# A graph network's edge phase on one core: first layer formed transposed in PSUM, the loop written out, one fp32 matmul for the segment sum

## What is computed

```python
edge_feat = jnp.concatenate([x[src], x[dst], edge_attr], axis=-1)   # 512 + 512 + 64
h = mish(edge_feat @ W1 + b1)                                       # x * tanh(softplus(x))
messages = mish(h @ W2 + b2)
agg = jax.ops.segment_sum(messages, dst, num_segments=x.shape[0])
```

## Time and profile before

| | |
|---|---|
| median of 3 runs | 1525.7 us (1524.73 to 1533.9) |
| the profiled execution's span | 1537.4 us, mean granted TensorE clock 0.889 |
| edge phase in it | from 116.4 us (L758, the table load) to 1176.9 us (first instruction of the node phase) |
| busy, whole span | PE 1222.1 us (79%), DVE 1091.5 (71%), ACT 895.1 (58%), POOL 923.7 (60%) |

### The profile page before, as it was taken

How to read it: one execution, slowest core, us unless ns; L and a number is a source line. 1 busy time by engine, 2 the same in 40 slices (tenths; PEclk the granted TensorE clock), 3 DMA queues, 4 the chain that set the end, 5 groups by cost and what they waited for, 6 DMA issues and landing times. The chain is left out here.

```text
span 1537.4 us, 21831 instructions
## 1 busy us (share of the span) xinstructions
PE 1222.1 (79%) x5491; PEld 929.1 (60%) x5492; DVE 1091.5 (71%) x1793; ACT 895.1 (58%) x1061; POOL 923.7 (60%) x1006
## 2 busy tenths in 40 slices
PE   0981788898888888888888888888894999559972
PEld 0751566666666666666666666666663777448861
DVE  3631587887988887888779777877887587663364
ACT  2211677777767776777677767767774454143341
POOL 1325687778778777887777878777743111064420
PEclk9995899989999999999899999989996999579975
DMA  4524444444444544544444444444431011363443
GB/s 135 198 103 89 103 95 94 95 83 101 87 88 91 96 89 84 100 95 87 96 88 92 98 87 87 91 91 93 90 82 55 8 40 43 103 162 114 130 150 119
DMA packets 113342, 147.33 MB, mean 96 GB/s; under 512 B 55389, under 2 KB 63980, under 8 KB 113225
## 3 DMA queue, kind: packets, MB, share of 16 engines
q0 software_dynamic: 40912, 101.69, 31.3%
q1 hardware_dynamic: 72377, 45.20, 10.7%
q10 hardware_dynamic: 16, 0.02, 0.0%
HBM read 136.29 MB, written 15.66 MB: 99 GB/s over the span
## 5 line engine op out<-in xcount | busy, mean ns | idle before, releaser
L896 PE MATMUL ps<-W2h,hTh 128*128 128x512 f32 x664 | 294.6, 444 | 74.5 <-ACT hTh L775 68.7
L730 POOL DMA_INDIRECT gath<-dst_table,idx_sl x166 | 285.1, 1718 | 41.7 <-issue 41.5
L896 PE MATMUL ps<-W2l,hTh 128*128 128x512 f32 x664 | 285.8, 430 | 0.0
L896 PEld LDWEIGHTS ps<-W2h,hTh 128*128 128x128 f32 x664 | 137.7, 207 | 138.8 <-ACT hTh L775 82.9
L718 POOL DMA_INDIRECT gath<-src_table,idx_sl x166 | 184.3, 1110 | 58.3 <-issue 55.2
L748 POOL TENSOR_TENSOR msg_lo<-act,msg_hi 128x1024 fp32r<-128x1024 f32 x83 | 199.6, 2404 | 31.3 <-DVE msg_hi L842 30.0
L769 ACT ACTIVATE act<-ps 128x1024 f32<-128x1024 f32 x83 | 85.0, 1024 | 206.8 <-POOL msg_lo L748 145.2
L866 DVE TENSOR_TENSOR agg<-agg,ps 125x512 f32 x166 | 113.7, 685 | 96.6 <-PE ps L940 85.6
L896 PE MATMUL ps<-W2h,hTl 128*128 128x512 f32 x664 | 168.3, 395 | 0.0
L706 POOL TENSOR_TENSOR e_carrier<-e_carrier 1x1 f32<-1x1 f32 x249 | 90.5, 363 | 119.6 <-DMA idx_sl<-idx_scr 88.9
L896 PEld LDWEIGHTS ps<-W2l,hTh 128*128 128x128 f32 x664 | 138.9, 209 | 30.5
(11 more groups left out here) (319 smaller groups left out, 2853.6 us busy)
## 6 DMA issues: line engine op xcount, KB each, us to landing
f_w_raw<-in_L_ffn_w_dram SPq DMA_DIRECT2D x32, 512.0 KB, 4.6
ea_sl<-ea_scr SPq DMA_DIRECT2D x166, 32.0 KB
ea_scr<-in_edge_attr_dram POOLq DMA_DIRECT2D x1, 5000.0 KB, 21.6
w_raw<-in_L_gnn_W_dram SPq DMA_DIRECT2D x3, 1024.0 KB, 18.7
idx_sl<-idx_scr SPq DMA_DIRECT2D x166, 1.5 KB
gath<-src_table,idx_sl POOLq DMA_INDIRECT x166
gath<-dst_table,idx_sl POOLq DMA_INDIRECT x166
x_raw<-in_x_dram SPq DMA_DIRECT2D x5, 500.0 KB
```

Source lines behind the costliest of these rows:

```text
L730: pool.indirect_dma_start(out=gath[:, kb, j, :], out_offset=None, in_=dst_table[:, :], in_offset=bass.IndirectOffsetOnAxis(ap=idx_sl[:, kb ...
L896: return nc.tensor.matmul(ps_2[:, kr, j, :], part[:, kr, j, d * P:(d + 1) * P], weights[:, d, :], start=False, stop=last)
```

## The change

Inside `edge_phase`:
- **First layer transposed.** `ps_1` gets a second slot and takes the transposed layout. PE transposes the gathered rows straight into it (8 transposes with `gath` as the stationary operand) and adds Wc by 8 matmuls of 256 columns, with `Wch`/`Wcl` stationary. `pre` and its addition on DVE are gone, and so is the transposition of h: exp and the product read `ps_1`, and the product is already transposed. `hTh` is a DVE copy, `hTl` a DVE subtraction of two SBUF tiles.
- **Segment sum.** `msg_hi` (DVE) and `msg_lo` (POOL) are gone; PE does one plain fp32 matmul a tile of `onehot` with `act2`. The one-hot matrix is one instruction a pair.
- **Who does what.** The copy to `eaT` moves from DVE to ACT, between the two Ln; the copy to `hTh` from ACT to DVE, before the second product.
- **Buffers.** Four for indices and attributes, three for `gath`, three for `act2`. The carrier instructions of POOL (L706) are gone.
- **Loop.** All 89 steps (-5 to `PAIRS` + 2) are straight code on every engine.
- The bias of the second layer uses 128 rows of `minus_r` and `bias_r` (zeros below row 2), where two rows were used; POOL clears the zeros at the start of the program. The other uses of both take rows 0 to 1 as before.

The diff, cut to its core (`...` marks what is left out; the removed lines of the engines' steps are those of the code above):

```diff
-        minus_r = sb("minus_r", [2, P], F32R)
+        minus_r = sb("minus_r", [P, P], F32R)
-        bias_r = sb("bias_r", [2, 4, HID], F32R)
+        bias_r = sb("bias_r", [P, 4, HID], F32R)
...
+            c.inc(nc.gpsimd.memset(f32(bias_r[:, 1, :]), 0.0))
...
+    IN, GA, E2 = 4, 3, 2 * P
...
-        pre = sb("pre", [P, 2, 2, HID])
+        eaT = sb("eaT", [2 * EDIM, 2, E2], F32R)
+        gath = sb("gath", [P, GA, 2, HID])
+        act1 = sb("act1", [P, 2, KC, E2])
+        act2 = sb("act2", [P, 3, 2, HID])
+        hTh = sb("hTh", [P, 2, KC, E2], F32R)
+        hTl = sb("hTl", [P, 2, KC, E2], F32R)
-        ps_h = ctx.enter_context(nc.psum_tensor("ps_h", [P, 2, HID], F32))
+        onehot = sb("onehot", [P, 2, 2, NE])
+        ps_1 = ctx.enter_context(nc.psum_tensor("ps_1", [P, 2, KC, E2], F32))
...
-        FIRST, LAST, LO, HI, UNROLL = -4, PAIRS + 3, 7, PAIRS - 5, 6
+        FIRST, LAST = -5, PAIRS + 2
...
+        def two_banks(k):
+            return ps_1[:, k].rearrange("p d e -> p (d e)").rearrange("p (j n) -> p j n", j=2)
...
-        dve_parts = {PAIRS + 1: (0, 1), PAIRS + 2: (2,), PAIRS + 3: (3, 4, 5, 6)}
+        dve_parts = {PAIRS + 1: (0, 1), PAIRS + 2: (2, 3, 4, 5, 6)}
...
         @block.sync
         def _(sp):
+            for s in range(FIRST, LAST + 1):
+                q = s + 5
+                if exists(q):
+                    k = q % IN
+                    if q >= IN:
+                        sp.wait_ge(*loaded(both_gath, GA, q - IN, 32))
+                        sp.wait_ge(S["split"], q - IN + 1)
+                        sp.wait_ge(S["dst_ready"], q - IN + 1)
...
         @block.gpsimd
         def _(pool):
+            for s in range(FIRST, LAST + 1):
+                b = s + 2
+                if exists(b):
+                    k = b % GA
+                    pool.wait_ge(*loaded(src_gath, GA, b, 32))
                     for j in range(2):
-                        pool.indirect_dma_start(out=gath[:, kg, j, :], out_offset=None, in_=src_table[:, :],
...
+                g = s + 3
+                if exists(g):
+                    k = g % GA
+                    pool.wait_ge(*loaded(idx_in, IN, g, 32))
+                    if g >= GA:
+                        pool.wait_ge(S["gath_read"], g - GA + 1)
...
         @block.scalar
         def _(act):
+            for s in range(FIRST, LAST + 1):
+                q, g, n = s, s - 2, s + 1
+                first, second = exists(q), exists(g)
+                a1, a2 = act1[:, q % 2], act2[:, g % 3]
+                if first:
+                    act.wait_ge(S["lin1_ps"], q + 1)
+                    if q >= 2:
+                        act.wait_ge(S["h_lo"], q - 1)
+                    nc.scalar.activation(a1, ps_1[:, q % 2], ACT.Exp).then_inc(S["exp1"], 1)
+                    act.wait_ge(S["lin2_ps"], g + 1)
+                    if g >= 3:
+                        act.wait_ge(S["sum_ps"], g - 2)
+                    nc.scalar.activation(a2, ps_2[:, g % 2], ACT.Exp, scale=-1.0).then_inc(S["exp2"], 1)
                 if first:
+                    nc.scalar.activation(a1, a1, ACT.Square).then_inc(S["sq1"], 1)
+                    act.wait_ge(S["inc2"], g + 1)
+                    nc.scalar.activation(a2, a2, ACT.Square).then_inc(S["sq2"], 1)
                 if first:
                     act.wait_ge(S["sq1"], q + 1)
+                    nc.scalar.activation(a1, a1, ACT.Ln, bias=half_col[:], scale=0.5).then_inc(S["ln1"], 1)
+                if exists(n):
+                    act.wait_ge(S["eaT_ps"], n + 1)
+                    if n >= 2:
+                        act.wait_ge(S["lin1_ps"], n - 1)
+                    nc.scalar.activation(eaT[:, n % 2, :], ps_1[:, n % 2, 0, :], ACT.Copy).then_inc(S["eaT_ready"], 1)
                 if second:
+                    act.wait_ge(S["sq2"], g + 1)
+                    nc.scalar.activation(a2, a2, ACT.Ln, bias=half_col[:], scale=0.5).then_inc(S["ln2"], 1)
                 if first:
                     act.wait_ge(S["ln1"], q + 1)
+                    nc.scalar.activation(a1, a1, ACT.Exp, scale=-1.0).then_inc(S["quot1"], 1)
                 if second:
+                    act.wait_ge(S["ln2"], g + 1)
+                    nc.scalar.activation(a2, a2, ACT.Exp, scale=-1.0).then_inc(S["quot2"], 1)
...
         @block.vector
         def _(dve):
...
+            for s in range(FIRST, LAST + 1):
+                q, r, g, a, n = s, s - 1, s - 2, s - 3, s + 2
+                if exists(q):
+                    dve.wait_ge(S["exp1"], q + 1)
+                    nc.vector.tensor_scalar(act1[:, q % 2], act1[:, q % 2], EXP_MAX, 1.0, ALU.min, ALU.add).then_inc(S["inc1"], 1)
+                if exists(g):
+                    dve.wait_ge(S["exp2"], g + 1)
+                    nc.vector.tensor_scalar(act2[:, g % 3], act2[:, g % 3], EXP_MAX, 1.0, ALU.min, ALU.add).then_inc(S["inc2"], 1)
+                if exists(a):
+                    for j in range(2):
+                        b = dve.value_load(block_i[0:1, a * 2 + j:a * 2 + j + 1], min_val=0, max_val=BLOCKS - 1)
+                        row = agg[:, bass.ds(b, 1), :].rearrange("p a d -> p (a d)")
+                        dve.wait_ge(S["sum_ps"], a + 1)
+                        if a * 2 + j > 0:
+                            dve.wait_ge(S["summed"], a * 2 + j)
+                        nc.vector.tensor_tensor(row, row, two_banks(a % 2)[0:NB, j, :], ALU.add).then_inc(S["summed"], 1)
+                if exists(r):
+                    nc.vector.tensor_tensor(hTl[:, r % 2], act1[:, r % 2], f32(hTh[:, r % 2]), ALU.subtract).then_inc(S["h_lo"], 1)
+                if exists(g):
+                    if g >= 2:
+                        dve.wait_ge(S["sum_ps"], g - 1)
+                    dve.wait_ge(S["dst_ready"], g + 1)
+                    nc.vector.tensor_tensor(onehot[:, g % 2], iota_n[:].unsqueeze(1).to_broadcast([P, 2, NE]),
+                                            dloc[:, 2 * g:2 * g + 2].unsqueeze(2).to_broadcast([P, 2, NE]), ALU.is_equal).then_inc(S["onehot_ready"], 1)
+                if exists(n):
+                    dve.wait_ge(*loaded(idx_in, IN, n, 32))
+                    nc.vector.tensor_tensor(dloc[:, 2 * n:2 * n + 2], idx_sl[:, n % IN, :, 2], block_off[:, 2 * n:2 * n + 2], ALU.subtract).then_inc(S["dst_ready"], 1)
+                if exists(q):
+                    dve.wait_ge(S["quot1"], q + 1)
+                    nc.vector.scalar_tensor_tensor(out=act1[:, q % 2], in0=act1[:, q % 2], scalar=1.0, in1=ps_1[:, q % 2],
+                                                   op0=ALU.subtract, op1=ALU.mult).then_inc(S["h_ready"], 1)
+                    dve.wait_ge(S["h_ready"], q + 1)
+                    if q >= 2:
+                        dve.wait_ge(S["lin2_ps"], q - 1)
+                    nc.vector.tensor_copy(hTh[:, q % 2], act1[:, q % 2]).then_inc(S["h_hi"], 1)
+                    dve.wait_ge(S["h_hi"], q + 1)
+                if exists(g):
                     dve.wait_ge(S["quot2"], g + 1)
+                    nc.vector.scalar_tensor_tensor(out=act2[:, g % 3], in0=act2[:, g % 3], scalar=1.0, in1=ps_2[:, g % 2],
                                                    op0=ALU.subtract, op1=ALU.mult).then_inc(S["msg_ready"], 1)
...
+                    return nc.tensor.matmul(ps_2[:, r % 2, j, :], part[:, r % 2, d, j * P:(j + 1) * P], weights[:, d, :], start=False, stop=last)
+                def hi_tile(j):
+                    nc.tensor.matmul(ps_2[:, r % 2, j, :], minus_r[:], bias_r[:, 1, :], start=True, stop=False)
+                    for d in range(KC):
+                        lin2(j, d, hTh, W2h)
+                        lin2(j, d, hTh, W2l)
+                if exists(m):
+                    o = two_banks(m % 2)
+                    pe.wait_ge(S["onehot_ready"], m + 1)
+                    pe.wait_ge(S["msg_ready"], m + 1)
+                    pe.wait_ge(S["h_ready"], min(s, PAIRS))
+                    for j in range(2):
+                        ins = nc.tensor.matmul(o[0:NE, j, :], onehot[:, m % 2, j, :], act2[:, m % 3, j, :], start=True, stop=True)
+                    ins.then_inc(S["sum_ps"], 1)
+                if exists(r):
+                    if r >= 2:
+                        pe.wait_ge(S["msg_ready"], r - 1)
+                    pe.wait_ge(S["h_hi"], r + 1)
+                    hi_tile(0)
+                    hi_tile(1)
+                if exists(n):
+                    k = n % 2
                     pe.wait_ge(S["split"], n + 1)
+                    if n >= 2:
+                        pe.wait_ge(S["h_ready"], n - 1)
+                    if n >= 4:
+                        pe.wait_ge(S["summed"], (n - 3) * 2)
                     for j in range(2):
+                        ins = nc.tensor.transpose(ps_1[:, k, 0, j * P:(j + 1) * P], f32(ea_hl[:, k, j, :]), ident[:])
                     ins.then_inc(S["eaT_ps"], 1)
...
+                if exists(r):
+                    pe.wait_ge(S["h_lo"], r + 1)
                     for j in range(2):
```

(24 more changed lines are left out.)

237 lines of the change are left out of this document (36 added, 201 removed).

## The result

| | before | after |
|---|---|---|
| median of the runs, on one chip | 1529.8 us (4 runs, 1524.7 to 1538.1) | 1641.5 us (4 runs, 1639.5 to 1641.9) |
| ratio | | 1.073 (1.067 to 1.079) |
| span of the profiled execution | 1537.4 us | 1639.7 us |
| mean granted TensorE clock in it | 0.889 | 0.870 |

The account below looks back on a forecast made before the run. A ring of TensorE, ACT and DVE bounds each step: 12.2 + 0.86 x 1.6 = 13.6 us. Over 79 steps +107 us, less 9 at the start: 1525.7 + 98 = 1624, taken as 1620 (range 1495 to 1640).

Parts of the forecast that it names:

- main case: Most edge steps at half clock after TensorE's stall: 13.6 us a step, 1590 to 1645 us; chance 0.52.
- the base: Time to which +98 us was added: the profiled execution's 1537.4 us, lowered by 11.7 to 1525.7.
- The ring: In the edge loop, TensorE, ACT and DVE wait for one another from sum to next sum: 12.2 us a step.
- The fp32 sum: TensorE's segment sum (L832), two plain fp32 matmuls of 512 columns at the start of a step: 1.9 us.
- The stall: TensorE stands still before the next segment sum (L832), from 10.2 to 12.2 us in every step: 2.0 us.
- What a fall costs: TensorE's matmuls after a stall run at half clock, which adds 1.6 us to the step.
- The share of falls: Share of steps whose TensorE stall is followed by half clock: 0.86, from 31 of 36 in the kernel before.
- Full clock: Rival: TensorE keeps its full clock in the edge steps, 12.2 us a step, 1512 us; chance 0.17.
- Every second step: Rival: about every second edge step has half clock, 13.0 us a step, 1576 us; chance 0.13.
- A ring that doesn't close: Rival: ACT or DVE has its input earlier, and TensorE's 10.0 us bounds the step: 1339 us; chance 0.05.
- The fetch of straight code: Rival: the edge loop's straight code is not fetched in time, 0.5 us or more a step: 1660 us; chance 0.06.
- the cheap sum: Rival: TensorE's fp32 sum at its lower bound, 0.9 us: 1545 us with half clock, 1434 without; chance 0.07.

## Why the prediction was off in its size

The direction and the mechanism came out: a ring through the `eaT` copy, as long as the step it replaced, and half clock on top. The time, 1641.5, lies 21.5 us above the forecast of 1620 and 1.5 above the upper end of the range, which stopped 5 us short of the prediction's own main case (1590 to 1645). The step that failed is the last one of the sum, the base to which the difference was added; the terms before it are off by 4 us in all. In order:

- **The ring** was forecast at 12.2 us. The kernel with eight more transposes shows it at full clock:

```profile
700.79 1.95 PE L832 MATMUL ps<-act,onehot 128*126 128x512 f32 x4 [1.19 <-issue]
...
706.78 0.38 PE L848 MATMUL ps<-ident,ea_hl 128*128 128x128 f32 x2
```

```profile
707.20 0.39 ACT L749 ACTIVATE eaT<-ps 128x256 fp32r<-128x256 f32 x1 [2.61 <-PE ps L848]
```

```profile
709.60 1.22 DVE L799 SCALAR_TENSOR_TENSOR act<-act,ps 128x1024 f32<-128x1024 f32 x1 [3.58 <-ACT act L755]
...
711.58 1.22 DVE L808 SCALAR_TENSOR_TENSOR act<-act,ps 128x1024 f32<-128x1024 f32 x1
```

  TensorE's part is 700.79 to 707.16, 6.4 us (6.5 forecast), ACT's 707.20 to 709.60, 2.4 (2.4), DVE's 709.60 to 712.80, 3.2 (3.15), 0.1 for the hand-over to TensorE at 712.90: 12.1.
- **The fp32 sum** takes 700.79 to about 702.58 (the first `hTh` matmul starts at 702.81, one bias of 0.23 lies before it), 1.8 us, where 1.9 was taken from the rows at half clock.
- **The stall**, 2.0 forecast, is 2.05. **What a fall costs**, 1.6: L848 starts 7.58 us after L832 in the changed kernel and 5.99 with eight more transposes, 1.59.
- **The share of falls** is the first term that was mis-sized: 0.86 was carried over from the kernel before, and 74 of 79 is 0.94. A shorter ring and a larger share nearly cancel, which is luck: the step was forecast at 13.6 and measured at 13.64, the marker's stretch at 1099 and 1101.
- **The start** came 6.9 us earlier, not 9.
- **The base is the step that failed.** Against the profiled execution's own 1537.4 us the sum gave 1635, 4 us under the measured span of 1639.7 (2 of the stretch, 2 of the start). I took off 11.7 us since the median of the runs was lower, and 4 more by taking 1620 for 1624; the last 2 us are that a run's time is longer than its span. That is the whole 21.5. The changed kernel's runs lie within 2.4 us, before's between 1515 and 1538, and before's profiled execution took longer than its fellows: its span of 1537.4 is above those of all 48 runs of before beside the experiments (1513.5 to 1535.6). Their granted clocks, whole spans, go with the time, 0.898 in the mean of the 12 fastest and 0.893 of the 12 slowest; the profiled execution has 0.889. So it had more half clock than most of them; the others have no trace to show where. That surplus is part of before's time alone. The steps of the changed kernel had been summed in full, from durations, so the 1099 us for the stretch was a figure of its own, and the median of before had nothing to correct in it.
- **The rivals.** Full clock (1512) is what four more transposes show, 1519.7; the kernel as changed is 0.4 us of stall away from it. Every second step (1576) is what two more transposes show, 1578.6. The prices were within 8 and 3 us, and the stall was known well enough to prefer the main case. A ring that doesn't close (1339) was made by moving the copy or the order, 1372.0 and 1374.2: the step is 10.2 to 10.3 there, not 10.0. The fetch of straight code is excluded by the loop written out, and the cheap sum by L832's 1.8 us.
- **The signs.** L808 every 13.6 us, 2 us of stall before L832, L799 behind L755 and the gathers (L704) behind L862 came as named. ACT's L749 waits 4.3 us for L848, not 2.5: the 2.61 above is the wait at full clock, and the 1.6 us by which half clock delays L848 had been left out. The mean granted clock is 0.870, not 0.85 or less.

The Trainium skill (TensorE: Matmul & The Clock Gate, "Why this matters for your kernels") asks for no pauses over about 3 us between bursts. The pauses here, 2.06 us, are shorter than that and cost the clock in 74 of 79 steps; the measurement decides.

## What to carry to other kernels

Before a small copy is moved to an engine with room, look at what stands behind it in that engine's queue: the copy took 0.4 us of ACT's idle time, but made an Ln and an exp wait for TensorE's middle, and that closed a ring which, with the half clock that it brought, cost 270 us. When rings are opened one at a time, the next one shows in who waits for whom, and two moves that are each worth much need not add up. Where TensorE stands still for a couple of microseconds in every step, an experiment with extra work behind the wait, work whose result is not needed, tells at once what the clock costs; and if a new step is summed from durations, its total stands for itself and is not shifted by the scatter of the old kernel's runs.

## What the runs showed of the hardware

- More work made the kernel faster: 0.44 us of transposes a step, 1641.5 to 1519.7 us.
- The share of stalls followed by half clock, by their length: 1.21 and 1.63 us none, 1.85 us 40 of 79, 2.06 us 74 of 79; but 44 of 79 for 2.06 us in a step that is 0.9 us shorter. In the changed kernel the five steps without a fall come 15 to 21 steps apart, and between them the four instructions of the sum get longer from step to step, from 2.4 us to 3.6, so more and more of the sum lies in the half clock. Then comes a step with none of it (1.95 us), as at 919.71:

```profile
645.05 2.38 PE L832 MATMUL ps<-act,onehot 128*126 128x512 f32 x4 [2.06 <-DVE act L808]
...
727.19 2.60 PE L832 MATMUL ps<-act,onehot 128*126 128x512 f32 x4 [2.06 <-DVE act L808]
...
905.95 3.60 PE L832 MATMUL ps<-act,onehot 128*126 128x512 f32 x4 [2.06 <-DVE act L808]
919.71 1.95 PE L832 MATMUL ps<-act,onehot 128*126 128x512 f32 x4 [2.06 <-DVE act L808]
931.82 2.42 PE L832 MATMUL ps<-act,onehot 128*126 128x512 f32 x4 [2.06 <-DVE act L808]
```

- A plain fp32 product with 512 columns takes 0.9 us (two instructions), one of fp32r 0.233, 3.8 times less. The Trainium skill (FP8 and Floating Point Precision, "TensorE Precision Notes") gives four passes for true fp32, and the trace agrees.
- DVE's cast to `hTh` (L804, 128 x 1024) lasts 0.693 to 0.695 us in the changed kernel and 0.693 to 0.969 in the one with the copy on DVE. Of the 34 that last 0.86 us or more, 32 start 0.57 to 0.67 us after the start of one of POOL's gathers (L694); most casts that start sooner or later after one last 0.69 to 0.70. Why is open:

```profile
L804 DVE CAST hTh<-act x83: 693/705/969, 142.2 to 982.7; 128x1024 fp32r<-128x1024 f32 x83
```
